# One expert projected without its gate weights in the routed layer of a four-layer kernel: expert 0 of the first half moved, the second half's norm moved

## The reference

```python
xn = x / norm(x);  logits = xn @ sn - sigmoid(gates)            # 16 experts
mask = relu(logits) > 0, with the two best where none is active
w = softmax(where(mask > 0, relu(logits), -inf))                # (tokens, 16)
def moe_proj(p): y = einsum('nc,ech->neh', x, p); return einsum('ne,neh->nh', w, y)
q, k, v = moe_proj(q_proj), moe_proj(k_proj), moe_proj(v_proj)  # p: (16, 256, 128)
attn = softmax(q @ k.T / sqrt(128));  o = attn @ v
out = einsum('enh,ehc->nc', einsum('ne,nh->enh', w, o), o_proj)
```

## Time and profile before

| | us |
|---|---|
| three runs | 593.52, 593.70, 598.35; median 593.7 |
| the profiled execution | 594.26, span 591.9 |
| PE busy | 575.5 |
| DVE busy | 385.2 |
| ACT busy | 219.4 |
| POOL busy | 137.1 |

### The profile page before, as it was taken

One profiled execution on the slowest core, in us unless ns is written; L12 is line 12 of the kernel. 1 busy time (PEld: TensorE's weight loads), 2 busy tenths in 40 slices (PEclk: granted clock), 3 DMA queues, 4 the chain that ended last, 5 costly groups with the idle time before them and its releaser, 6 DMA issues.

```text
span 591.9 us, 10358 instructions
## 1 busy us (share of the span) xinstructions
PE 575.5 (97%) x3971; PEld 426.4 (72%) x3971; DVE 385.2 (65%) x928; ACT 219.4 (37%) x513; POOL 137.1 (23%) x172
## 2 busy tenths in 40 slices
PE   9999999999999999999999989998999999999997
PEld 7766344444456767999999748777878888887687
DVE  1996667687886755222222679986999779775454
ACT  3554666666673374221222376684200010001000
POOL 0053101113005202222221000004355555440000
PEclk9999999999999999999999999999999999999999
DMA  8920000002001653999996100700733652320000
GB/s 189 306 113 1 18 2 1 31 8 57 2 1 28 212 208 111 334 337 336 349 357 237 55 2 1 243 7 3 275 108 107 223 214 83 105 81 0 1 28 29
DMA packets 25694, 71.07 MB, mean 120 GB/s; under 512 B 5270, under 2 KB 13062, under 8 KB 21814
## 3 DMA queue, kind: packets, MB, share of 16 engines
q1 hardware_dynamic: 21910, 58.15, 29.7%
q0 software_dynamic: 3744, 12.38, 6.2%
HBM read 65.02 MB, written 5.49 MB: 119 GB/s over the span
## 4 chain that ended last, share of the span: by engine, by line
PE 77%; DVE 15%; ACT 6%; issue 1%; POOL 0%; DVEq 0%; POOLq 0%
PE bank L2194 12%; PE bank L1665 9%; PE bank L2000 8%; PE bank L2013 8%; PE bank L1820 7%; PE bank L2272 7%; PE bank L2182 7%; PE bank L1794 4%; PE bank L1838 3%; ACT region L1554 2%; PE bank L1763 2%; PE bank L1826 2%; ACT region L1560 1%; DVE nmax L1062 1%; DVE umax L690 1%
## 5 line engine op out<-in xcount | busy, mean ns | idle before, releaser
L2194 PEld LDWEIGHTS bank<-region,kvT 128*128 128x128 f32 x448 | 77.0, 190 | 10.0 <-issue 0.9
L2194 PE MATMUL bank<-region,kvT 128*128 128x200 f32 x448 | 81.2, 333 | 0.8 <-DVE region L1179 0.8
L762 DVE TENSOR_REDUCE nmax<-bank 100x2 f32<-100x722 f32 x64 | 55.2, 905 | 29.9 <-PE bank L1794 29.8
L2000 PEld LDWEIGHTS bank<-stage,region 128*128 128x128 f32 x448 | 52.1, 192 | 1.4 <-issue 0.8
L2000 PE MATMUL bank<-stage,region 128*128 128x128 f32 x448 | 52.4, 275 | 0.5 <-ACT stage L1489 0.5
L2013 PE MATMUL bank<-region,stage 128*128 128x256 f32 x224 | 50.7, 380 | 0.0
L2182 PE MATMUL bank<-region,kvT 128*128 128x400 f32 x128 | 48.4, 502 | 1.3 <-DVE region L1186 1.3
L2013 PEld LDWEIGHTS bank<-region,stage 128*128 128x128 f32 x224 | 41.5, 190 | 5.1
L2272 PE MATMUL bank<-region,kvt 128*128 128x200 f32 (+1 forms) x192 | 44.5, 389 | 0.3 <-DVE region L1246 0.3
L976 DVE TENSOR_SCALAR stage<-bank,stage 128x128 f32<-128x128 f32 x56 | 15.8, 344 | 44.2 <-PE bank L2000 44.2
L1512 ACT ACTIVATE stage<-bank,stage 128x128 f32<-128x128 f32 x56 | 16.0, 368 | 67.2 <-PE bank L2000 41.5
(11 more groups left out here) (360 smaller groups left out, 1089.8 us busy)
## 6 DMA issues: line engine op xcount, KB each, us to landing
region<-in_e_w SPq DMA_DIRECT2D x28, 1024.0 KB, 5.1
kvT<-in_p_qkv SPq DMA_DIRECT2D x32, 384.0 KB, 3.1
stage<-w_dram POOLq DMA_DIRECT2D x2, 1600.0 KB, 13.9
stage<-in_t_f SPq DMA_DIRECT2D x1, 2048.0 KB, 16.0
kvt<-in_p_o SPq DMA_DIRECT2D x1, 2048.0 KB, 10.2
stage<-in_e_b SPq DMA_DIRECT2D x14, 128.0 KB, 6.5
region<-in_ctxT SPq DMA_DIRECT2D x3, 541.5 KB, 14.1
stage<-w_dram POOLq DMA_DIRECT2D x3, 400.0 KB, 5.4
```

Source lines behind the costliest of these rows:

```text
L762: dve.tensor_reduce(nmax[:, b % 2, at_h:at_h + 9:8], banks[0:N, bank:bank + 2, 0:M], AX.X, ALU.max, negate=True)\
L2000: ins = pe.matmul(psum[2 * u + m // 4][:, (m % 4) * P:(m % 4 + 1) * P], e_w1[u][:, k, m * P:(m + 1) * P], xsT[u][:, k, :], start=k == 0, s ...
L2194: return pe.matmul(bank, left, right, start=e == 0 and i % 2 == 0, stop=e == E1 - 1 and i in (1, 3, 5, 6))
```

## The change

Expert 0 of half 0 is projected without weights: six matmuls of 400 columns (q, k and v by two blocks of channels) of the plain xT into banks 0, 1 and 2, in the place of the filler. Five stand before the weights are waited for, the sixth behind the spread of expert 1 and the turn, which change places. ACT copies the three results to `plain`, a part of kvt. DVE multiplies them by expert 0's weight behind expert 13 (weigh_plain) and adds them to the joined q, k and v behind expert 4 of half 1 (add_plain). The products in seven parts and their banks begin with expert 1. POOL forms no sums for n = 0. The experts spread by PE are 1 and 2, both through bank 5. The groups of w_bc for half 0 become 1, 4, 8 and 3 experts. The norm of half 1 goes behind expert 5 on DVE, gate_logits(1) behind 8, gate_weights(1) behind 10; on PE turn_half(1) behind 5, gate_scores(1) behind 6, turn_weights(1) behind 10. POOL forms sums up to n = 12 (13 before) ahead of the second half's broadcast. The attention of half 0 stands four experts later in half 1.

```diff
-GROUPS = (((2, 4), (4, 8), (8, 16), (0, 2)), ((0, 2), (2, 8), (8, 16)))
+GROUPS = (((3, 4), (4, 8), (8, 16), (0, 3)), ((0, 2), (2, 8), (8, 16)))
...
+        def projected(n):
+            return n + PLAIN
+        def summed(n):
+            return 4 * n - 2
...
-                    sp.wait_ge(S["qkv_mm"], n - NP + 1)
+                    sp.wait_ge(S["qkv_mm"], projected(n - NP))
...
-                for n in range(NP) if h == 0 else range(NP, E1 - 2):
+                for n in range(1, NP) if h == 0 else range(NP, E1 - 3):
                     sum_weights(n)
...
-                if h == 0 and e < 2:
-                    dve.wait_ge(S["w0_mm"], e + 1)
-                    for ks in (slice(0, 1), slice(1, 2)) if e == 0 else (slice(0, 2),):
+                if h == 0 and e < 3:
+                    dve.wait_ge(S["w0_mm"], e)
+                    for ks in (slice(0, 1), slice(1, 2)) if e == 1 else (slice(0, 2),):
...
+            def add_plain():
+
+                dve.wait_ge(S["qkv_out"], PLAIN + 3)
+                dve.tensor_tensor(qkv_cols[0], qkv_cols[0], plain, ALU.add).then_inc(S["qkv_out"], 1)
+
+            def weigh_plain():
+
+                dve.wait_ge(S["qkv_out"], PLAIN)
+                dve.wait_ge(S["wb_first"], 16)
+                link(dve.tensor_tensor(plain, plain, w_bc[0][:, None, 0, :].to_broadcast([P, PLAIN, HT]), ALU.mult))
...
-            weigh_tokens(0, 0)
-            sum_tokens(0, 0)
-            weigh_tokens(0, 1)
-            sum_tokens(0, 1)
+            for e in range(1, 3):
+                weigh_tokens(0, e)
+                sum_tokens(0, e)
             third_residual(1)
             last_variance(1)
-            weigh_tokens(0, 2)
-            sum_tokens(0, 2)
-            last_normalise(1)
-            token_norm(1)
             for e in range(3, E1):
                 weigh_tokens(0, e)
                 sum_tokens(0, e)
-                if e == 4:
+                if e == 5:
+                    last_normalise(1)
+                    token_norm(1)
+                if e == 8:
                     gate_logits(1)
-                if e == 6:
+                if e == 10:
                     gate_weights(1)
+                if e == 13:
+                    weigh_plain()
             for e in range(E1):
...
                 if e == 4:
+                    add_plain()
+                if e == 8:
                     attention_maxima(0)
-                if e == 5:
+                if e == 9:
                     attention_norm(0)
...
+            def plain_out(j):
+
+                act.wait_ge(S["qkv_mm"], j + 1)
+                act.copy(plain[:, j, :], psum[j][:, 0:HT]).then_inc(S["qkv_out"], 1)
...
+            def project_plain():
+
+                pe.wait_ge(S["p_in0"], 16)
+                for j in range(PLAIN):
+                    for k in range(2):
+                        if (j, k) == (2, 1):
+                            spread_weights(1)
+                            turn_weights(0)
+                        ins = pe.matmul(psum[j][:, 0:HT], p_w[0][:, k, j * HE:(j + 1) * HE], xT[:, k, 0:HT],
+                                        start=k == 0, stop=k == 1)
+                    ins.then_inc(S["qkv_mm"], 1)
...
-            keep_busy(0, 7)
-            turn_weights(0)
-            spread_weights(0)
-            for e in range(E1):
-                if e == 0:
+            project_plain()
+            for e in range(1, E1):
+                if e == 1:
                     project_first()
                 else:
                     project(0, e)
-                if e == 2:
+                if e == 5:
                     turn_half(1)
-                if e == 3:
+                if e == 6:
                     gate_scores(1)
-                if e == 9:
+                if e == 10:
                     turn_weights(1)
```

More of the change, by code:

```diff
@@ L50 @@
 RESULT = ((0, 0), (1, 0), (2, 0), (3, 0), (6, 0), (6, D), (7, 0), (7, D))
-GROUPS = (((2, 4), (4, 8), (8, 16), (0, 2)), ((0, 2), (2, 8), (8, 16)))
+GROUPS = (((3, 4), (4, 8), (8, 16), (0, 3)), ((0, 2), (2, 8), (8, 16)))
 QT = HT // 2
-SPREAD_BANK = (5, 3)
+SPREAD_BANK = 5
+FIRST_SUM = (1, 0)
+PLAIN = 3
 GATE_BANK = (4, 5)
@@ L268, in cut_r @@
             return region[:, at_r[0] - n:at_r[0]]
+        plain = kvt_region[:, E1 * D:E1 * D + PLAIN * HT].rearrange("p (j t) -> p j t", j=PLAIN)
         x_w = [cut_r(2 * HT).rearrange("p (k t) -> p k t", k=2) for _ in range(NW)]
         z_w = [cut_r(HT) for _ in range(NW)]
-        qkvT = [[cut_r(HT) for _ in range(3)] for _ in range(2)]
+        qkv_cols = [cut_r(3 * HT).rearrange("p (j t) -> p j t", j=3) for _ in range(2)]
+        qkvT = [[qkv_cols[h][:, j, :] for j in range(3)] for h in range(2)]
         v_tok = cut_r(4 * HE)[0:N].rearrange("p (b h) -> p b h", b=4)
@@ L571, in _ @@
                         .then_inc(S[f"wb_in{h}{g}" if g < 3 else "wb_first"], 16)
-            for n in range(E1 - 2, 2 * E1):
+            for n in range(E1 - 3, 2 * E1):
                 sum_weights(n)
@@ L1582, in gates @@
                 act.activation(soft[:, bs, :], soft[:, bs, :], ACT.Exp).then_inc(S["lg_exp"], 1)
+                if h == 0:
+                    for j in range(2):
+                        plain_out(j)
                 act.wait_ge(S["wT_mm"], h + 1)
                 act.copy(wT[:, h * HT:(h + 1) * HT], psum[GATE_BANK[h]][0:E1, 0:HT]).then_inc(S["wT_out"], 1)
+                if h == 0:
+                    plain_out(2)
             def projections_out(h):
-                act.wait_ge(S["qkv_mm"], E1 * (h + 1))
+                act.wait_ge(S["qkv_mm"], projected(E1 * (h + 1) - 1))
                 for i in range(2):
@@ L2182, in whole @@
                     ins = pe.matmul(psum[V_BANK[h]][:, 0:HT], p_w[n % NP][:, k, 2 * HE:3 * HE], x_w[n % NW][:, k, :],
-                                    start=e == 0 and k == 0, stop=e == E1 - 1 and k == 1)
+                                    start=e == FIRST_SUM[h] and k == 0, stop=e == E1 - 1 and k == 1)
                 return ins
@@ L2193, in part @@
                          x_n[:, 1, QT:HT])[i]
-                return pe.matmul(bank, left, right, start=e == 0 and i % 2 == 0, stop=e == E1 - 1 and i in (1, 3, 5, 6))
+                return pe.matmul(bank, left, right, start=e == FIRST_SUM[h] and i % 2 == 0, stop=e == E1 - 1 and i in (1, 3, 5, 6))
             def project_sums(h, e):
                 n = E1 * h + e
-                pe.wait_ge(S["pool_step"], 3 + 3 * (n + 1))
+                pe.wait_ge(S["pool_step"], 3 * n + 3)
+                if n == 1:
+                    pe.wait_ge(S["qkv_out"], 2)
@@ L2208, in project_first @@
             def project_first():
-                pe.wait_ge(S["p_in0"], 16)
+                pe.wait_ge(S["p_in1"], 16)
+                pe.wait_ge(S["qkv_out"], 1)
                 pe.wait_ge(S["xw_done"], 1)
-                part(0, 0, 0)
-                spread_weights(1)
-                pe.wait_ge(S["xw_done"], 2)
+                part(0, 1, 0)
+                spread_weights(2)
                 pe.wait_ge(S["wT_out"], 1)
-                whole(0, 0)
-                part(0, 0, 1)
-                project_sums(0, 0)
@@ L2219, in project_first @@
-                pe.wait_ge(S["xw_done"], 6)
-                part(0, 0, 6).then_inc(S["qkv_mm"], 1)
+                whole(0, 1)
+                part(0, 1, 1)
+                project_sums(0, 1)
+                part(0, 1, 6).then_inc(S["qkv_mm"], 1)
             def project(h, e):
```

53 lines of the change are left out of this document (31 added, 22 removed).

## The result

The changed kernel takes 590.53 us (median of 15 runs, 589.63 to 594.16), the kernel before 594.49 in the same comparison (15 runs, 593.02 to 598.35): ratio 0.994, 95% interval 0.9926 to 0.9955. It is faster by 0.6%, about 4 us; 588.6 and a gain of 5.1 were forecast. In two later calls it came out at ratios 0.9931 (0.9905 to 0.9957) and 0.9932 (0.9909 to 0.9956). The time lies in the range of 587.6 to 590.8. But most of the chance (0.77) stood on "same", on the ground that a measurement "tells about 1% from no change". The interval is 0.3% wide in all, and 0.6% is a clear gain, not an equality.

A forecast was written before the change was run, and what follows sets the result against it. PE, busy 575.5 of 591.9 us, was taken as the bound. Gains 4.1 + 1.6 = 5.7, less 0.3, 0.1, 0.1 and 0.1, gave 5.1: 593.7 - 5.1 = 588.6 us, range 587.6 to 590.8.

The forecast's parts named there:

- the one thing that is later: Half 0's weight broadcasts: turn behind spread, POOL issues at about 415.9, not 415.06; cost 0 to 0.7, taken as 0.3.
- A measurement of this kernel tells about 1% from no change: Whole time: 1% is 5.9 us, border 587.8; faster 0.18, same 0.77, slower 0.05.
- rival 3: DVE becomes the bound of the half, its experts stretched by POOL's sums: 597.3 us, slower; chance 0.05.
- What bounds the kernel: Whole kernel: PE busy 575.5 of 591.9 us; time is won by removing matmuls or closing PE's few waits.
- The gates' stand: PE before half 0's experts: ten plain rows, 3.35 us, cost nothing; the last matmul fills 0.76 us of idle time.
- Gain so far 4.1: Half 0: one expert less on PE, 3.71 us, plus 0.38 from DVE's list starting earlier.
- At most one POOL instruction, some 0.4 us: DVE's tokens of expert 3 beside POOL's sums for expert 4: loss of at most one POOL instruction, some 0.4 us.
- The norm and the logits: Half 1's norm and logits on DVE, moved later: PE's wait before expert 5, 1.37 plus 0.24 restart, goes; gain 1.6.
- the slack at expert 9: After the moved logits, DVE has tokens of expert 9 at 446.0 against PE's 446.6: slack of 0.6 us.
- rival 2: Expert saved, but the logits' wait only moves as DVE's slack at expert 9 is used up: 590.0 us; chance 0.17.
- hidden, 0 to 0.3: DVE weighs the plain product behind expert 13 and adds it in half 1: 1.5 us each, hidden, bound 0 to 0.3.
- Rival 1: Transfers decide: second broadcast group and loads behind it come late, PE stands 3.0 us: 591.6 us; chance 0.12.

The follow-up runs named there:

- e1: Kernel before with only the moves of half 1's norm, logits and weights, expert 0 still weighted: 593.32 us, ratio 0.9986 to the kernel before.
- the two controls: The changed kernel, unedited, measured twice more beside edited kernels: 590.72 us, ratio 0.9931, and 590.32 us, ratio 0.9932, to the kernel before.

## Why the prediction was right or wrong

The prediction named the right gains, and what failed is the price of "the one thing that is later", with a term that it left out, POOL's queue in front of expert 13. Its range held partly by luck: a gain of 0.8 that it had not priced made up for a part of what it missed.

- **"A measurement of this kernel tells about 1% from no change"** failed. It had three runs of one kernel behind it; 15 runs against 15 give an interval of 0.9926 to 0.9955. The forecast gain itself, 5.1 of 593.7, is 0.86%, and it was put with "same", while rival 3's loss of 0.6% was put with "slower".
- **What bounds the kernel** held: PE at 97%, and every microsecond of the ruler is a matmul gone or a wait of PE.
- **The gates' stand** held on PE: ten rows for nothing, the 0.76 of idle time filled, the first part at once behind the plain matmul. It left out DVE: the sums that go with expert 0 free it by 0.2 to 0.8 there, 0.8 between these two profiles. That was a gain I had not priced.
- **"Gain so far 4.1"** failed by its second term. The expert of 3.71 came; the 0.38 by which DVE's list starts earlier became a loss of 0.62. Tokens of expert 3 waited 0.50 for the first group and then took 1.20, beside POOL's sums for expert 4. "At most one POOL instruction, some 0.4 us" was about right for that instruction: 0.2.
- **"The one thing that is later"** is the step that was mis-sized. I had the groups leave at 415.9, "the load for expert 4 may add 0.3". The load, 0.09 ahead of the store, added 1.1, and the groups left 4.1 us after the start of ACT's copy and not 3.0 (417.58 - 413.45; 415.06 - 412.02 before). My price for the second group then was right (it took 7.8 and not 8.3). The cost was 0.3 by the forecast; waits of 0.90 and 0.17 with their restarts, part of them against a gain counted before, it was about 1.4.
- **The norm and the logits** held: the wait went, the slack at expert 9 was there, and rival 2 (the wait stays) and rival 3 (DVE becomes the bound) were wrong. e1 shows the gain alone, 1.4 and not 1.6: the 0.24 of restart was the difference of two durations whose ends are modelled, and between starts a restart costs 0.07 (3.79 for the next expert and not 3.71). Rival 2's 590.0 is the nearest number to the gain measured, 3.7 against 4.0, and that is luck: its wait is not in the changed kernel.
- **A term was missing:** POOL's queue in front of expert 13. I had followed POOL's order for half 0 and not for half 1, where the change moves the sums of 13 behind the broadcasts and puts a 1.39 us DVE instruction in their way. It cost 0.98 in this profile and 0.4 in the two controls, and the second store, which lands just behind a load as the first does, is a part of it.
- **The weighing of the plain product "hidden, 0 to 0.3"** was right for DVE's own time and wrong for what it blocks.
- **Rival 1**, that transfers decide, was right as a mechanism and had the wrong transfer: not the group's or the next load's length, but the 25 KB store in front.
- The sum: 5.7 less 0.6 was forecast. Measured on the ruler: 5.7 + 0.8 for the stand - 1.0 for expert 3 (0.90 of wait and what was to come early) - 0.4 for expert 4 - 1.0 for expert 13 - 0.2 for the restart priced too high = 3.9. In the two controls it is 4.5 and 4.6. So 5.1 was 0.5 to 1.2 too much.

The Trainium skill's rule on the port that DVE and GpSimd share ("SBUF — State Buffer", "Who interferes with whom") was used for one instruction of 0.4 us. The prediction gave it without its condition: an instruction with one SBUF input is free of the port only outside the 2-port perf modes. The 0.43 above has one SBUF input and ended at 408.48, just behind POOL's subtraction (407.99 to 408.45), so "never" was too wide; whether it ran in such a mode no run here shows. By the same rule the first sum for expert 13 had to wait out the rest of the weighing: 1.39 - 0.18 = 1.21 and then its own 0.72, 1.93; it took 1.79, and in the controls 1.92 and 1.85 where the same sum gives 2.06 and 2.01. The traces agree within 0.16, and the rule would have found the term that was missing.

## What to carry to other kernels

When work is put ahead of a small transfer on a serial path (copy, store, reload), look at which larger transfer now leaves just before it: here a load released more than 4 us earlier put 1.1 us on a 25 KB store that everything waited for. Follow each engine's queue through every place where the change reorders it, the second half as well as the first. And when a wait is removed behind an engine that has slack, ask who was using that slack: here a gain of 1.1 to 1.4 was real and was used up by two waits that the earlier order had not had. And price a restart between starts, not by durations with modelled ends.

## What the runs showed that was not expected

The store of the turned weights takes 2.0 us with the load behind it and 3.0 to 3.2 with the load just ahead of it, in all profiles of half 0. In half 1, with a load 1.1 to 1.4 us ahead of it, it took 2.1 to 3.4, always landing just behind that load. DVE and POOL, both reading SBUF, cost each other whole instructions: 1.79 to 1.92 where 0.72 is usual, 1.51 and 1.54 where 0.98 is usual; so the sums of one expert dropped from POOL shorten a stretch that holds only small DVE steps by 0.2 to 0.8.
